# Two launch queues for the bulk weight and activation loads of an attention and feed-forward layer on eight cores

## What is computed

```python
q = (x @ Wq.T + bq).reshape(B, T, 16, 128).transpose(0, 2, 1, 3)
k = x @ Wk.T + bk
v = x @ Wv.T + bv
scores = where(pos_s < pos_t, einsum('bhtd,bsd->bhts', q, k) / sqrt(128), -1e30)
attn = softmax(scores) * row_valid
x = layernorm(x + einsum('bhts,bsd->bhtd', attn, v).reshape(B, T, 2048) @ Wo.T + bo)
hidden = fwht(silu(x @ W1.T) * (x @ W3.T))
x = layernorm(x + hidden @ W2.T)
```

## Time and profile before

| what | us |
|---|---|
| median of 2 runs | 2863.22 (2855.25 to 2871.18) |
| profiled execution | 2876.03 |
| its span on the slowest core (core 1) | 2874.5 |
| spans of the 8 cores | 2838.0 to 2874.5 |
| PE busy | 2439.3 (85%) |
| ACT busy | 653.4 (23%) |
| DVE busy | 546.5 (19%) |
| POOL busy | 162.1 (6%) |
| matmuls of line 177, 128x512 on loaded weights | 2081.2 |

### The profile page before, as it was taken

One profiled execution on the slowest core, in us unless ns is written; L12 is line 12 of the kernel. 1 busy time (PEld: TensorE's weight loads), 2 busy tenths in 40 slices (PEclk: granted clock), 3 DMA queues, 4 the chain that ended last, 5 costly groups with the idle time before them and its releaser, 6 DMA issues.

```text
span 2874.5 us, 27907 instructions; the slowest of 8 cores (2838.0 to 2874.5 us)
## 1 busy us (share of the span) xinstructions
PE 2439.3 (85%) x10080; PEld 910.8 (32%) x10080; DVE 546.5 (19%) x760; ACT 653.4 (23%) x1107; POOL 162.1 (6%) x304
## 2 busy tenths in 40 slices
PE   3888857888999997956999999999999998979793
PEld 1223311111122122323444444444444443434341
DVE  1111256544332331131000000000000000010002
ACT  1222223445556551043111111111111100000001
POOL 1111101100000000000000000000000000000000
PEclk9679957888999998977999999999999999989896
DMA  8864563321000001113222222222222144546453
GB/s 246 226 181 142 172 192 117 97 91 33 1 1 1 1 1 59 59 67 109 69 71 67 74 66 67 73 66 70 70 67 73 52 133 138 150 133 206 134 153 125
DMA packets 96461, 276.70 MB, mean 96 GB/s; under 512 B 11716, under 2 KB 11844, under 8 KB 91976
## 3 DMA queue, kind: packets, MB, share of 16 engines
q0 software_dynamic: 37968, 156.26, 18.4%
q1 hardware_dynamic: 58360, 118.65, 13.1%
HBM read 224.54 MB, written 50.33 MB: 96 GB/s over the span
## 4 chain that ended last, share of the span: by engine, by line
PE 77%; DMA 7%; ACT 6%; DVE 5%; issue 4%; DVEq 0%; ACTq 0%; POOL 0%; SPq 0%; POOLq 0%
PE pb L177 75%; DMA GA<-XBT 2%; PE pb L179 2%; DMA GA<-X1S 2%; ACT GA L427 2%; DVE pb L424 1%; ACT GA L664 1%; ACT GA L240 1%; DMA W2P<-GA 1%; DVE GA L244 1%; DVE GA L465 1%; DMA GA<-W2P 1%; ACT GA L552 1%; ACT GA L559 1%; DVE GA L724 0%
## 5 line engine op out<-in xcount | busy, mean ns | idle before, releaser
L177 PE MATMUL pb<-GA 128*128 128x512 bf16 x8576 | 2081.2, 391 | 227.1 <-ACT GA L427 51.7
L177 PEld LDWEIGHTS pb<-GA 128*128 128x128 bf16 x8576 | 799.2, 99 | 1364.0 <-issue 569.8
L427 ACT ACTIVATE GA<-pb 128x512 bf16<-128x512 f32 x576 | 340.9, 597 | 334.2 <-PE pb L177 232.2
L177 PE MATMUL pb<-GA,CB 128*1 128x512 bf16 (+1 forms) x704 | 276.0, 407 | 2.8 <-DVE GA L644 2.8
L664 ACT ACTIVATE GA<-pb 128x512 bf16<-128x512 f32 x128 | 69.6, 594 | 840.8 <-PE pb L177 840.8
L644 DVE TENSOR_TENSOR GA<-GA,pb 128x512 bf16<-128x512 f32 x128 | 82.3, 683 | 913.1 <-ACT GA L641 883.8
L179 PE MATMUL pb<-GA,CB 64*64 64x512 bf16 x512 | 109.7, 449 | 80.1 <-ACT GA L240 52.4
L177 PEld LDWEIGHTS pb<-GA,CB 128*1 128x1 bf16 (+1 forms) x704 | 58.0, 82 | 280.6 <-issue 265.8
L424 DVE TENSOR_TENSOR pb<-pb,GA 128x512 f32<-128x512 f32 x128 | 88.6, 698 | 296.9 <-PE pb L177 289.5
L244 DVE CAST GA<-pb 128x512 bf16<-128x512 f32 x128 | 82.5, 686 | 286.7 <-PE pb L179 271.4
L724 DVE TENSOR_TENSOR GA<-pb,GA 128x512 f32<-128x512 f32 x32 | 20.6, 686 | 498.3 <-PE pb L177 435.0
(11 more groups left out here) (47 smaller groups left out, 389.7 us busy)
## 6 DMA issues: line engine op xcount, KB each, us to landing
GA<-W2P SPq DMA_DIRECT2D x256, 256.0 KB, 2.6
GA<-W2T POOLq DMA_DIRECT2D x128, 256.0 KB, 5.0
W2P<-GA SPq DMA_DIRECT2D x128, 256.0 KB, 5.6
GA<-W1S POOLq DMA_DIRECT2D x64, 512.0 KB, 3.8
GA<-W3S POOLq DMA_DIRECT2D x64, 512.0 KB, 3.8
GA<-XBT POOLq DMA_DIRECT2D x8, 2048.0 KB, 16.9
GA<-WQS POOLq DMA_DIRECT2D x4, 2048.0 KB, 12.4
GA<-XOWN SPq DMA_DIRECT2D x1, 8192.0 KB, 36.0
```

The costliest lines, as they stand in the source:

```text
L177: return e.matmul(out, lhsT, rhs, start=start, stop=stop, skip_group_check=True)
L427: texp = em.op("s", lambda e, qp=qp, slot=slot: e.activation(pbuf[slot], qp[:], AF.Exp, scale=SC), waits=_mx(dep, pbuf_rd[slot]))
```

## The change

Seventy loads are appended to SP's list in place of POOL's: those of XBT for the odd blocks 1, 3, 5 and 7, of WQS for groups 1 and 3, and all 64 of W3S. Their waits, buffers and sizes stay, and so does all compute. The code below a changed line moves down by one or two lines.

```diff
@@ -273,7 +273,8 @@
         for blk in range(8):
             sl = blk % 2
             src = XBT.rearrange("(c p) s -> p c s", p=128)[:, :, blk * 512:blk * 512 + 512]
-            tl = em.op("g", lambda e, sl=sl, src=src: e.dma_start(
+            tl = em.op("g" if blk % 2 == 0 else "y",
+                       lambda e, sl=sl, src=src: e.dma_start(
                 xtb[sl].rearrange("p (c s) -> p c s", c=16), src),
                 waits=_mx(xtb_rd[sl]))
@@ -334,7 +335,8 @@
         for oq in range(4):
             sl = oq % 2
-            tl = em.op("g", lambda e, sl=sl, oq=oq: e.dma_start(wqb[sl], WQS[oq]),
+            tl = em.op("g" if oq % 2 == 0 else "y",
+                       lambda e, sl=sl, oq=oq: e.dma_start(wqb[sl], WQS[oq]),
                        waits=_mx(wq_rd[sl]))
@@ -603,7 +605,7 @@
             tl1 = em.op("g", lambda e, sl=sl, tau=tau: e.dma_start(w1b[sl], W1S[tau]),
                         waits=_mx(w1_rd[sl]))
-            tl3 = em.op("g", lambda e, sl=sl, tau=tau: e.dma_start(w3b[sl], W3S[tau]),
+            tl3 = em.op("y", lambda e, sl=sl, tau=tau: e.dma_start(w3b[sl], W3S[tau]),
                         waits=_mx(w3_rd[sl]))
```

## The result

The changed kernel takes 2979.64 us (median of 11 runs) against 2875.62 us for the kernel before (10 runs, the earlier ones among them). The ratio is 1.0417, with a 95% interval of 1.0368 to 1.0467: slower by 4.2%, where 2980 us and 4.1% were forecast. The profiled execution took 2979.68 us.

The account below looks back on a forecast made before the run. TensorE, with line 177 matmuls 75% of the chain of waits, was taken as the bound, copies mostly hidden. K/V +85.1, Q +31.8 and feed-forward 0 gave +116.9 us on the 2863.2 us median: 2980 us, range 2925 to 3023 us.

Parts of the forecast that it names:

- The step in the list: K/V stage: odd XBT copies wait behind W2P stores on SP, starting 2.2 us after TensorE runs dry.
- The landing: K/V stage: odd and even XBT copies land together, 5.24 MB at 237 GB/s, 22.1 us a pair; block 7 14.0 us.
- The blocks: K/V stage: a block takes 17.4 us after a wait, and 16.7 us for even blocks without one.
- WQS: Q stage: two moved copies each make TensorE wait 14.6 us, with a 1.3 us slow restart each; +31.8 us in all.
- W3S: Feed-forward stage: the moved copies have 19 us of slack and SP is idle, so 0 us.
- the rival: K/V and attention stages: TensorE's rests buy a higher clock, returning 81 us; +36 us, 2899 us, within 2%; chance 0.05.
- The rings get in each other's way: K/V and Q stages: an XBT pair takes 33.8 us; +160 us in all, 3023 us; chance 0.13.
- Much faster copies: K/V and Q stages: an XBT pair lands in 15.3 us, blocks take 14.7 us; +67 us, 2930 us; chance 0.16.
- the K/V term: K/V stage: seven blocks after the first take 208.8 us in place of 123.7 us, +85.1 us.
- the Q term: Q stage: two exposed copies and the slow restarts after them add +31.8 us.

Follow-up runs that it names:

- The two experiments on place and on stores: Place: changed kernel, odd XBT and WQS loads listed ahead of stores, ratio 1.0029. Stores: changed kernel without W2 steps in K/V blocks, 1.0033; kernel before likewise, 0.9925.

## Why the prediction was right

**The step in the list.** The prediction said that the odd copies would be launched 2.2 us after the even block ends. They are launched at 52.25 - 49.97 = 2.3 us. Four waits beside the opening one, none before even blocks, two more for WQS: all as forecast. The K/V stage ends at 250.5 us on core 7 and 253.6 us on core 1, where 259 was named. The two experiments on place and on stores show that it is the place that does it.

**The landing.** A pair was to take 22.1 us. From launch to the block's first matmul it is 76.72 - 52.25 = 24.5, 133.75 - 110.20 = 23.6, and 21.5 us for the third; the waits are 26.7, 25.9 and 24.3 us against 24.3 forecast, 4.0 us more in all. Block 7 waited 17.6 us against 16.2. The way to it, bytes over the rate of the busy stretch, held in the main: during the first two waits the DMA engines moved 224 and 232 GB/s in place of 237, some 5.4 to 5.5 MB in place of 5.24 (core 7, stretches of the waits, and then of two blocks that follow):

```profile
52.30:76.60 24.30, 0.00 (x0) 0.00 (x0) 0.00 (x0) 0.00 (x0) 0.50 (x1) 0.50 0.86 224
110.00:133.60 23.60, 0.00 (x0) 0.00 (x0) 0.00 (x0) 0.00 (x0) 0.70 (x1) 0.50 0.90 232
...
76.70:107.80 31.10, 25.40 (x104) 9.74 (x104) 4.39 (x7) 8.03 (x14) 3.08 (x6) 0.83 0.28 70
```

**The blocks, mis-sized.** The term that was too large is the length of a block. I took 17.4 us for a block after a wait and 16.7 for the next, from core 1, whose granted clock was 0.70 in that stage. On core 7 they took 16.2, 15.0 and 15.9, and 15.0, 13.4 and 14.9 us: the granted clock of the first two is 0.83. That is 12.0 us less in the three pairs, and block 7 another 1.7. So from the end of block 0 to the end of block 7 there are 250.5 - 50.0 = 200.5 us, in place of the 208.8 forecast and the 123.7 of before: +76.8 us where +85.1 stood. The longer landings took 5.4 us of what the faster blocks gave.

It was not the change that made core 7's blocks short. In the kernel before, this core had a granted clock of 0.86 in the K/V stage and needed 157.17 - 48.35 = 108.8 us for the seven blocks, 5.1 us of it waits: 14.8 us a block, where core 1 needed (123.7 - 9.0) / 7 = 16.4. After the change core 7's blocks average 15.1 us. Each core against itself, the stretch of seven blocks grew by 91.7 us on core 7 and by 204.2 - 123.7 = 80.5 us on core 1. On core 1 they average 15.7 us, 0.7 less than before. The term was taken from one core of one execution, and two cores of that execution differ by 1.6 us a block, where the forecast was 2.0 us too long on core 7 and 1.4 on core 1.

**WQS.** Two waits of 15.4 and 14.1 us, 29.5 together, against 29.2. The restarts cost 10.00 - 7.08 and 8.88 - 7.08, 4.7 us together, against 2.6. But the stage grew by only 448.71 - 255.17 - (344.89 - 178.90) = 27.5 us, not 31.8 (178.90 and 255.17 us are the first matmuls of the two Q stages). The first group gives back the difference: its granted clock over the 45 us from its start is 0.92 now (core 7), and was 0.77 before (core 1):

```profile
255.17:300.00 44.83, 35.64 (x160) 14.31 (x160) 5.15 (x8) 9.14 (x16) 4.09 (x8) 0.92 0.38 114
```

```profile
178.90:226.00 47.10, 42.35 (x158) 15.73 (x158) 3.68 (x6) 9.14 (x16) 3.62 (x7) 0.77 0.48 146
```

Each core against itself, the stage from its first matmul to the start of attention grew by 23.6 us on core 1, by 32.0 us on core 7 and by 27.9 us as a mean over the eight.

**W3S.** Forecast at 0, measured at 1.0006 alone.

**The rivals.** Against the lengths that the forecast took from core 1, some 14 us came back in the K/V blocks and 7 in the Q stage. How much of it the pauses gave is small or unclear: the K/V stage without its waits for XBT is 123.3 us as a mean over the cores, against 126.3 before; on cores 0 to 3 it fell from 131.4 to 123.5, on cores 4 to 7 it rose from 121.2 to 123.1. And nothing came back where the rival needed it. Over the first 371 us of attention the granted clock is 0.77, as before, now in the first fence and before in the second:

```profile
448.70:820.00 371.30, 289.17 (x893) 60.93 (x893) 196.94 (x240) 153.23 (x266) 30.66 (x60) 0.77 0.37 113
```

```profile
344.90:716.00 371.10, 290.58 (x895) 61.08 (x895) 197.24 (x241) 153.22 (x266) 30.66 (x60) 0.77 0.37 113
```

That stage shows no trace of the pauses. "The rings get in each other's way" falls with the 24 us of a pair, which is what shared bandwidth gives. "Much faster copies" falls with the same number. **The sum.** Forecast +116.9 us. The ratio of 1.0417 on the 2863.22 us that the forecast was set on is +119 us (its interval +105 to +134); between the slowest spans of the two profiled executions it is +103.5 us, since that of before lay 12.8 us above this median. So the time of 2980 us was met more closely than the terms deserve: against the same profile the K/V term was 8.3 us and the Q term 4.3 us too large, and that match also crosses from core 1 to core 7. Each core against itself, the mean growth is 110.0 us: 79.9 in the K/V stage (85.1 forecast), 27.9 in the Q stage (31.8) and 2.2 behind them (0). The mechanism and the size hold; that the total came out at 2980 us is luck.

## What to carry to other kernels

Before moving a launch to another engine's list, write down what stands ahead of it there and what that waits for: a load put behind stores of the work it should be hidden by can no longer be hidden, and each one costs its landing time in full. Splitting loads over two lists bought nothing even with free places, since the same DMA engines serve both; move a launch for its place, not for the queue. Where a transfer becomes exposed, size it as the bytes that are in flight together over the rate of a busy stretch, and take compute times from several cores: in one and the same profile a K/V block took 16.4 us on core 1 and 14.8 us on core 7.

## What was not expected of the hardware

In one execution, and at the same work, the granted TensorE clock of the K/V stage differed between cores by more than the change altered it. In the kernel before it was 0.70 on core 1, and on core 7:

```profile
48.30:157.20 108.90, 83.85 (x366) 32.85 (x364) 18.36 (x29) 28.11 (x49) 22.07 (x35) 0.87 0.86 266
```

In the changed kernel the three pairs of blocks behind pauses of 25 us ran at 0.84, 0.80 and 0.86 on core 1, and at 0.83, 0.95 and 0.83 on core 7. The second pair on core 7:

```profile
133.70:162.20 28.50, 22.24 (x104) 9.02 (x104) 4.38 (x7) 8.03 (x14) 3.08 (x6) 0.95 0.29 80
```

There the 32 matmuls of block 4 took 7.08 us at 148.77 us, where on core 1 before the change the blocks from block 3 on had taken 9.3 to 10.1 us. But core 7 had such a block before the change as well, behind a wait of 0.35 us:

```profile
124.41 7.07 PE L177 MATMUL pb<-GA 128*128 128x512 bf16 x32 [0.35 <-DMA GA<-XBT]
```

So on core 1 the clock was higher after the change and on core 7 it was not, on the whole; what makes the difference between the cores was not tried. In the pauses themselves it is 0.50, its lower level of 1.2 GHz, as the stretches of core 7's first two waits, under "The landing", show. Not expected either was that packing the 1 KB runs of XBT into 16 KB rows, which raised the rate of a burst from 237 to 278 GB/s, would leave the time of the kernel before at 1.0005.
